# A state-space convolution taken batch by batch between the searches of a cross attention

## The reference

```python
scores = einsum('bthd,bghd->bhtg', x @ Wq, ctx @ Wk) / sqrt(32)      # 4 heads, 64 context rows
topv, topi = top_k(scores, 32)                                       # the search
attn_mean = zeros.at[topi].set(softmax(topv)).mean(axis=heads)
c_t = attn_mean @ (ctx @ Wv)
x = layernorm(x_text, g_norm_in, b_norm_in)
scale_in, shift_in = split(c_t @ W_film_in + b_film_in)
x = x * (1 + mod_gate * scale_in) + mod_gate * shift_in              # "film"
y = irfft(rfft(x, 1024) * Kf)[:512] + x * D_skip                     # s4d, along the 512 tokens
scale_out, shift_out = split(c_t @ W_film_out + b_film_out)
xt = x_text + y * (1 + mod_gate * scale_out) + mod_gate * shift_out
```

## Time and profile before

| | us |
|---|---|
| median of 3 runs (3710.67 to 3717.41) | 3711.43 |
| profiled execution | 3717.24 |
| its span, first to last instruction | 3715.2 |
| TensorE busy in the span | 2823.8 (76%) |
| VectorE | 2403.8 (65%) |
| ScalarE | 1112.4 (30%) |
| GpSimd | 990.2 (27%) |

### The profile page before, as it was taken

The page is one execution under the profiler, slowest core; times in us unless marked ns, Lnnn a source line. Parts: engine busy times, 40 slices in busy tenths (PEclk is TensorE's granted clock), DMA queues, the critical chain, the costliest instruction groups (busy, mean ns, idle before and its releaser), DMA issues. The chain is left out here.

```text
span 3715.2 us, 40807 instructions
## 1 busy us (share of the span) xinstructions
PE 2823.8 (76%) x11784; PEld 1837.2 (49%) x11784; DVE 2403.8 (65%) x7562; ACT 1112.4 (30%) x2880; POOL 990.2 (27%) x1221
## 2 busy tenths in 40 slices
PE   4754896399956767776777678756467889999999
PEld 2322564277743445544554456434433446666666
DVE  4995564455321799989989998999757425212112
ACT  1112562133302333443343334332232023221221
POOL 2550000300030345454544454445422210000000
PEclk7555997699956678787868786866777999999999
DMA  2000002355522221221122112211020041212212
GB/s 90 0 0 15 6 1 82 130 161 169 155 81 74 83 80 41 84 63 67 53 73 72 59 54 70 64 55 33 5 77 1 0 97 59 67 52 74 67 52 68
DMA packets 180762, 235.36 MB, mean 63 GB/s; under 512 B 35761, under 2 KB 138869, under 8 KB 180286
## 3 DMA queue, kind: packets, MB, share of 16 engines
q1 hardware_dynamic: 177470, 224.37, 19.1%
q0 software_dynamic: 3072, 8.39, 0.7%
HBM read 170.57 MB, written 62.13 MB: 63 GB/s over the span
## 5 line engine op out<-in xcount | busy, mean ns | idle before, releaser
L2063 DVE MATCH_REPLACE8 a_rest<-a_best,a_rest 128x416 f32<-128x416 f32 (+54 forms) x1308 | 602.9, 468 | 0.0
L2071 DVE MAX8 a_best<-a_rest 128x8 f32<-128x416 f32 (+54 forms) x1308 | 564.3, 472 | 0.0
L1746 PE MATMUL a_pat<-a_kp,a_probs 128*128 128x128 f32 x1344 | 290.6, 390 | 203.7 <-POOL a_kp L1965 198.4
L1746 PEld LDWEIGHTS a_pat<-a_kp,a_probs 128*128 128x128 f32 x1344 | 258.1, 287 | 285.9 <-POOL a_kp L1965 262.8
L2004 POOL TENSOR_SCALAR a_probs<-a_mixed,a_best 128x120 f32<-128x120 f32 (+12 forms) x208 | 285.6, 1373 | 331.2 <-DVE a_best L2075 303.4
L1727 PE MATMUL a_psc<-a_kT,branch 64*128 64x264 f32 (+3 forms) x640 | 227.7, 613 | 161.7 <-ACT a_stage L1829 160.9
L3174 DVE TENSOR_TENSOR tl_hT<-tl_act_out,tl_gate 128x512 f32<-128x512 f32 x128 | 88.6, 692 | 385.9 <-ACT tl_act_out L3042 385.8
L1737 PE MATMUL a_pmix<-a_rows,a_kpre 128*128 128x264 f32 (+41 forms) x528 | 187.2, 485 | 84.9 <-ACT a_mixed L1862 80.1
L1727 PEld LDWEIGHTS a_psc<-a_kT,branch 64*128 64x128 f32 x640 | 119.4, 262 | 252.0 <-ACT a_stage L1829 226.8
L2956 PE MATMUL tl_py<-tl_w,tl_hT 128*128 128x256 f32 x1024 | 241.6, 379 | 0.0
L2937 PE MATMUL tl_ph<-xT,tl_w 128*128 128x512 f32 x512 | 240.7, 592 | 0.0
(11 more groups left out here) (418 smaller groups left out, 5267.2 us busy)
## 6 DMA issues: line engine op xcount, KB each, us to landing
f_w<-in_L_ffn_W SPq DMA_DIRECT2D x39, 1024.0 KB, 5.8
tl_gate<-l_gates SPq DMA_DIRECT2D x256, 128.0 KB, 2.9
l_scores<-a_stage SPq DMA_DIRECT2D x32, 528.0 KB, 2.7
l_scores<-a_stage SPq DMA_DIRECT2D x32, 400.0 KB, 2.4
l_scores<-a_stage SPq DMA_DIRECT2D x32, 272.0 KB, 2.1
f0o_w<-in_L_ffn_W SPq DMA_DIRECT2D x8, 1024.0 KB, 12.5
sorted_x<-z_blank SPq DMA_DIRECT2D x1, 4992.0 KB, 15.6
f_xs<-sorted_x SPq DMA_DIRECT2D x39, 128.0 KB, 5.4
```

What stands on the lines that cost most here:

```text
L1746: ins = pe.matmul(pat[:, at + c, :], probs[:, g % 4, c * P:(c + 1) * P], kp[:, g % 4, :], start=True, stop=True)
L2063: last[a] = signal(dve.match_replace(rest[:, a, 0:wd], best[:, a, q - 1, :], rows_of[a] if q == 1 else rest[:, a, 0:wd], GONE))
L2071: last[a] = signal(dve.max(best[:, a, q, :], rest[:, a, 0:wd]))
```

## The change

- The convolution is taken by batch `b`, not by pair: `forward(b, m)` puts the real and the imaginary part of 256 columns each into the two halves of a bank (8 products of 256 columns); `backward(b, j)` makes one tile (8 products of 256 columns, always into the first `po` bank) and with it the film-out product (one of 512 columns, into the second).
- Batch `b` is transformed forward in TensorE's turn `u = 2b + 2` and backward in `u = 2b + 3`; so batches 0 to 2 lie beside rounds 2 to 7, and batch 3 behind round 7.
- `film(u-1)` stands ahead of `scores(u+1)` on TensorE. On VectorE it stands one search later in odd rounds.
- On ScalarE, exponential 0 and hats 0 stand ahead of the eight evacuations of `vw`.
- GpSimd's combines and skips follow their new places; `spec`, `prod`, `y`, `t` and `sk` are half as large.

In the diff, TensorE's functions and turn come first, then ScalarE's opening, then VectorE's functions and round.

```diff
-                def forward(p, m, c):
+                def forward(b, m):
...
-                        pe.wait_ge(pm_dve, TT // 2 * (p + 1))
-                    for k in range(NT):
-                        ins = pe.matmul(pf[n % 2][:], dft[:, k, f:f + P], pair(G.branch, p, k),
+                        pe.wait_ge(pm_dve, NT * (b + 1))
+                    for c in range(2):
+                        for k in range(NT):
+                            f = (c * FT + m) * P
+                            ins = pe.matmul(pf[n % 2][:, c * D:(c + 1) * D], dft[:, k, f:f + P], G.branch[:, b * NT + k, :],
...
+                def backward(b, j):
+                    n, i = item(b, j, 0), b * NT + j
                     if n >= 2:
                         pe.wait_ge(o_read, n - 1)
                     if j == 0:
+                        pe.wait_ge(ready, FT * (b + 1))
                     for m in range(2 * FT):
+                        ins = pe.matmul(po[n % 2][:, 0:D], inv[:, m, j * P:(j + 1) * P], spec[:, m, :],
                                         start=(m == 0), stop=(m == 2 * FT - 1))
                     ins.then_inc(o_full, 1)
+                    if n >= 2:
+                        pe.wait_ge(o_read, n)
+                    pe.matmul(po[(n + 1) % 2][:], mT[:, i * P:(i + 1) * P],
+                              vw[:, b, 2:4, :].rearrange("p i d -> p (i d)"), start=True, stop=True).then_inc(o_full, 1)
...
                 for u in range(UNITS + 1):
                     if u >= 1:
                         mean(u - 1)
+                        film(u - 1)
                         if u + 1 < UNITS:
                             scores(u + 1)
-                        film(u - 1)
-                    if UNITS // 2 <= u < UNITS:
+                    if u >= 2:
                         for r in range(4):
-                            first_half(u - UNITS // 2, r)
+                            if u % 2 == 0:
+                                forward(u // 2 - 1, r)
+                            else:
+                                backward(u // 2 - 1, r)
...
                 queries(1)
+                act.wait_ge(again_ready, 1)
+                exponential(0)
+                hats(0)
                 act.wait_ge(film_in, 16 * (4 + 2 * B))
...
+                def product(b, m):
+                    x = pf[n % 2][:].rearrange("p (c d) -> p c d", c=2)
+                    k = kf[:].rearrange("p (c m) d -> p m c d", c=2)[:, m]
+                    dve.tensor_tensor(prod[:, n % 2, 0], x, k, ALU.mult)
+                    dve.tensor_tensor(prod[:, n % 2, 1], x, k[:, ::-1, :], ALU.mult).then_inc(xread, 1)
+                def result(b, j):
+                    dve.tensor_tensor(y[:, s], po[n % 2][:, 0:D], sk[:, s], ALU.add).then_inc(o_read, 1)
+                    step(dve.tensor_tensor(t[:, s], po[(n + 1) % 2][:, 0:D], y[:, s], ALU.mult))
+                    dve.tensor_tensor(t[:, s], po[(n + 1) % 2][:, D:2 * D], t[:, s], ALU.add).then_inc(o_read, 1)
+                    dve.tensor_tensor(G.branch[:, i, :], t[:, s], G.x[:, i, :], ALU.add)
+                def piece(u, r):
+                    if u >= 2:
+                        (product if u % 2 == 0 else result)(u // 2 - 1, r)
...
                     left = search(u, 0, None)
+                    piece(u - 1, 3)
                     left = search(u, 1, left)
-                    if u >= 1:
+                    if u >= 2 and u % 2 == 0:
                         film(u - 1)
                     left = search(u, 2, left)
+                    if u % 2 == 1:
+                        film(u - 1)
+                    piece(u, 0)
                     left = search(u, 3, left)
+                    piece(u, 1)
                     average(u, left)
+                    piece(u, 2)
```

More of the change, by code:

```diff
@@ L2159, in reads_through, with item @@
             return sum(by_dve(x) == by_dve(uses[u]) for x in uses[:u + 1])
[L2161 to L2171, removed]
+        def item(b, j, r):
+            return 2 * (b * NT + j) + r
         with nc.Block() as block:
@@ L2328, in _ @@
                         mean(u - 1)
+                        film(u - 1)
                         if u + 1 < UNITS:
                             scores(u + 1)
-                        film(u - 1)
-                    if UNITS // 2 <= u < UNITS:
+                    if u >= 2:
                         for r in range(4):
-                            first_half(u - UNITS // 2, r)
-                for m in range(FT):
-                    for c in range(2):
-                        forward(1, m, c)
+                            if u % 2 == 0:
+                                forward(u // 2 - 1, r)
+                            else:
+                                backward(u // 2 - 1, r)
                 for j in range(NT):
-                    backward(1, j)
-                    film_out(1, j)
+                    backward(B - 1, j)
             @block.gpsimd
@@ L2377, in skips @@
[L2377 to L2380, removed]
-                        pool.wait_ge(conv_in, 64)
[L2382 to L2399, removed]
+                def combine(b, m):
+                    n = b * FT + m
+                    pool.wait_ge(xread, n + 1)
+                    if b and m == 0:
+                        pool.wait_ge(o_full, item(b - 1, NT - 1, 0) + 1)
+                    pr = prod[:, n % 2]
+                    pool.tensor_tensor(spec[:, m, :], pr[:, 0, 0, :], pr[:, 0, 1, :], ALU.subtract)
+                    pool.tensor_tensor(spec[:, FT + m, :], pr[:, 1, 0, :], pr[:, 1, 1, :], ALU.add).then_inc(ready, 1)
@@ new lines, in skips @@
+                def skips(b, j):
+                    i = b * NT + j
+                    pool.wait_ge(pm_dve, NT * (b + 1))
+                    if i == 0:
+                        pool.wait_ge(conv_in, 64)
+                    if i >= 2:
+                        pool.wait_ge(o_read, 2 * i - 3)
+                    pool.tensor_tensor(sk[:, i % 2, :], G.branch[:, i, :], skip[:], ALU.mult).then_inc(skipped, 1)
+                for u in range(UNITS + 1):
+                    if u < UNITS:
+                        gains(u)
+                    if u >= 2 and u % 2 == 0:
+                        for m in range(FT):
+                            combine(u // 2 - 1, m)
+                        skips(u // 2 - 1, 0)
+                        skips(u // 2 - 1, 1)
+                    elif u >= 2:
+                        skips(u // 2 - 1, 2)
+                        skips(u // 2 - 1, 3)
@@ L2401, in _ @@
+                skips(B - 1, 2)
+                skips(B - 1, 3)
             @block.scalar
@@ L2529, in film @@
                         dve.tensor_tensor(x, x, pm[n % 2][:, D:2 * D], ALU.add).then_inc(pm_dve, 1)
-                def product(p, m, c):
-                    n, s = bank(p, m, c), (p * FT + m) % 2
+                def product(b, m):
+                    n = b * FT + m
                     dve.wait_ge(xfull, n + 1)
[L2534 to L2542, removed]
@@ L2544, in result @@
-                def result(p, j):
-                    n, s = item(p, j, 0), (p * NT + j) % 2
-                    dve.wait_ge(o_full, n + 1)
[L2547 to L2555, removed]
+                    if n >= 2:
+                        dve.wait_ge(ready, n - 1)
```

81 lines of the change are left out of this document (17 added, 64 removed).

## The result

The changed kernel took **3688.92 us**, the median of 5 runs (3670.57 to 3693.1). The kernel before, timed on the same chip in turn with it, took 3711.43 (5 runs, 3703.7 to 3720.45). The ratio is **0.9923, interval 0.9907 to 0.9938**: faster, by 0.8%. The forecast was 3667, range 3658 to 3682. The sign was right, the gain about half of what was forecast, and the time lies outside the range. The profiled execution took 3693.1 (span 3691.3), 24.1 less than the profiled one before (3717.24).

What follows compares the result with a forecast made beforehand. No engine was full in the stage; TensorE would bound its rounds and convolution. Opening 2, round 1 4, the rest from later rounds and a tail of 37 instead of 70: 3711.4 - 44.2 = 3667 us, range 3658 to 3682.

Steps and rivals of the forecast that it cites:

- For the clock 2.0: Rounds and tail: 2.0 us allowed for TensorE slowing behind gaps, 1 us in the tail and one in the rounds.
- The gaps cool TensorE: Rival, rounds and tail: each of eight gaps costs 1.6 to 1.9 us of slowed TensorE, kernel at 3679; chance 0.10.
- The opening: Exponential 0 moved ahead: search 1 at 2754.05 instead of 2756.12, gain 2.07 us, bounds 0.5 to 2.6.
- The table load hides under that wait: Opening, ScalarE: the table load, to 2734.7, runs while exponential 0 waits for the peak, which comes at 2735.1.
- Round 1: Film ahead of the next scores on TensorE: the round lasts 15.5 us in place of 19.5, gain 4.
- First forward: Start of the first forward transform: 2782.0, taken between 2779.7 at full clock and 2784.3 at half clock.
- The narrow matmul halves: Convolution on TensorE: a 256-column record takes 0.216 us where a 512-column one takes 0.433.
- The wide-as-long rival: Convolution: a 256-column record takes 0.433 us, as long as the wide one, +111, kernel 3778; slower at all: chance 0.03.
- The pair of rounds 46.6, third pair 42.4: Rounds 2 to 7, bound by TensorE: 46.6 us per pair including waits, 42.4 for the third, which lacks some scores.
- GpSimd's contention: Rounds: GpSimd slowing VectorE, 32 small operations at up to 0.72 = 23 us; shares the present-habit rival's chance 0.07.
- The rounds keep their present habit: Rival, rounds 2 to 7: three quarters of the convolution cost 54 us over six such rounds, gain 21, kernel 3690; chance 0.07.
- What would show it: Listed trace signs; wrong if records over 0.25, clock under 0.9 in rounds 3 to 7, later peaks several us, pair over 50.

Runs made afterwards that it cites:

- the scores first: Changed kernel with TensorE taking the next scores between mean and film in rounds 3 and 5: 3632.52 us, ratio 0.9884 to the kernel before.
- the repeat: The changed kernel timed and profiled again with no edit: median 3647.05 us, ratio 0.9924 to the kernel before.
- film behind: Changed kernel with film put back behind the next scores on TensorE in every round: 3637.97 us, ratio 0.9895 to the kernel before.
- the opening undone: Changed kernel with exponential 0 and its hats back behind the eight film-weight evacuations: 3639.86 us, ratio 0.9909 to the kernel before.
- The kernel with the pieces: All repairs together, but scores 1 evacuated before the film weights and exponential 0 in pieces between the evacuations: 3615.57 us, ratio 0.9839 to the kernel before.

## Why the prediction was wrong, step by step

- **"For the clock 2.0": the failed step.** 18.2 were paid. The first forward, begun cold, cost 2.05 (16.13 - 14.08). In round 3, film to the end of its first backward tile took 12.67 (2805.15 to 2817.82), where full clock takes 7.78 (2756.23 to 2764.01 with useless products): 4.9. Round 5 took the same 12.67: 4.9. Round 7, without scores, took 8.65 in place of 5.3: 3.4. The tail's first backward tile took 6.66, where it took 3.69 behind the same gap with the scores first: 3.0. That is 16.2 of the 21.9 by which the stage ended later than forecast. The rows of before showed one slow group behind a gap, 1.5 to 1.9 over its full-clock time, and I took that as the price of a gap. It was the price of a clock that stayed down for 3 us; in the changed kernel it stayed down for 7 to 10, with film, scores and a backward tile behind each other on the engine that bounds the rounds. Why it stayed down longer is open. The rival "The gaps cool TensorE" named the mechanism but gave it the same price, 1.6 to 1.9 a gap, for all eight gaps, and a chance of 0.10. In the trace it was four stretches at 3.0 to 4.9 and the cold start, while the even rounds (gap 0.97) never fell. Useless products in the gaps took the falls away.
- **The opening: the gain did not come.** Forecast 2.07 gained; in this profile search 1 came 2.1 late (2758.26 against 2756.12), and in none of the six with this opening was it more than 0.7 earlier after the keys than in the profile before (40.1 against 40.8). "The table load hides under that wait" fell: it is issued with the first exponential and waited for the peak too (idle 1.91, then 1.28). So the third weight product began at 2739.17 + 0.85 = 2740.0, where the forecast said 2738.65, TensorE idle 3.77, and its 24 records took 13.46 (10.48 in the repeat). The lower bound of 0.5 excluded what came. The Trainium skill's page "ScalarE: Activation LUTs" (What ACT_TABLE_LOAD costs) puts a drain beside each load. In this trace none stands behind the load (2734.35 to 2735.63, first exponential at 2735.64); one ahead of it could hide in the idle 1.91, but the kernel before, with 0.02 us between copy and load, shows none.
- **Round 1: right, and better.** 13.6 from search to search (2757.41 to 2771.02) where 15.5 was forecast: the film's waits were nearly gone.
- **First forward: 1.9 later behind search 2 than forecast.** I took the middle between full and half clock for films and scores 3; they ran at half clock (film 3.78, scores 1.22 per pair of records).
- **The narrow matmul halves: right**, 0.220 a record in 64. The wide-as-long rival is dead.
- **The pair of rounds 46.6, third pair 42.4: right at full clock**, 46.9 twice and 42.9 with three useless products. With the gaps filled the whole kernel's ratio was 0.9877, where the forecast's own was 3667 / 3711.4 = 0.9880. That it is so close is partly luck: the stage was 40.5 shorter than before (282.4 - 241.9), not 44.
- **GpSimd's contention: did not come.** No peak but the first was slowed (0.16 each, 8.70 the first), though the page "GPSIMD Engine Reference" of the Trainium skill (Key points) had given reason to weigh it. "The rounds keep their present habit" gave 3690 by another mechanism and nearly the measured time; the useless products exclude it, since they leave VectorE and GpSimd as they were.
- **What would show it**: "clock under 0.9 in rounds 3 to 7" and "a pair over 50" were written as signs of a wrong forecast, and both came, the first narrowly (0.89 from 2801 to 2931).

**Left open**: why a given gap is followed by a fall. The same 1.78 in round 7 cooled TensorE in the changed kernel (both profiles) and with film behind, not with scores first nor with the opening undone; the 2.95 of the tail did so in three kernels and not in two; two falls came with no gap. The page "TensorE: Matmul & The Clock Gate" (HAM oscillation — how this bites in real kernels) of the Trainium skill describes waits for DMA between groups, after which each group starts cold. The trace agrees only in part: a wait stood before most falls, each of which cost 3.0 to 4.9 us, but in the changed kernel film in round 3 began at full clock (1.00 in 2805 to 2806) and the clock fell under it. These rows don't let one say beforehand which gap it will be, nor how long the clock stays down: with film behind the scores it was 3 us in the forward of batch 1 and 7 in that of batch 3, each behind a wait of 1.27.

## What to carry to other kernels

When an edit makes TensorE the bound, go through its queue for idle stretches between thin products and price each not as the gap but as everything that follows on that engine at half clock: here 3 to 5 us for a gap of 1.8 to 3. Put required work in the gap where the order allows it (that brought 14 us), and useless products where it doesn't (18 us with twelve of them). An instruction moved ahead brings its wait and its table load in front of all that is queued behind it; cut it into pieces between that work instead of moving it whole. The kernel with the pieces, whose next scores also went ahead, had the lowest median of all.

## What the hardware showed that I had not expected

- Useless work made the kernel faster: 3628.74 against 3647.05 on one chip.
- Gaps of 0.97 us in even rounds and of 0.72 left by one product were never followed by a fall; those of 1.78 in odd rounds mostly were, and a TensorE with no idle time ran at 0.59 for 6 us.
- The table load begins only when the wait of the activation behind it is over (peak ready at 2734.26, load at 2734.35).
- Where the clock fell behind a wait of 2 to 4 us in the kernel before, it was down for 3 us; in the changed one, behind 1.8 to 3, it was down for 7 to 10.
- The spread of one program's executions goes with the clock: of five runs of the changed kernel, the fastest (3670.57) had a mean granted clock of 0.821, the others (3683.47 to 3693.1) 0.813 to 0.817.
